# State-space rows turned by a DMA transpose of 16 bit word planes in place of TensorE transposes

## What is computed

```python
x = x + 0.5 * ffn(layernorm(x), W_up, W_gate, W_down)     # ternary weights, silu(up) * gate, 2048 hidden
x = x + mamba(layernorm(x), W_in, conv_w, conv_b, W_out, A_log, D_param, dt_bias)
x = x + 0.5 * ffn(layernorm(x), W_up, W_gate, W_down)
```

```python
S = S * dA_t + dt_t * outer(x_t, B_t)
y_t = S @ C_t
y = (y + D * x) * silu(z)
out = y @ W_out.T
```

## Time and profile before

| | us |
|---|---|
| median of 3 runs | 1743.13 (1742.04 to 1743.46) |
| the profiled execution, its own time | 1743.55 |
| its span, first to last instruction | 1741.8 |
| PE busy | 1707.3 |
| DVE, ACT, POOL busy | 1300.9, 880.5, 743.1 |
| the state-space stage | about 626 to 1135 |

### The profile page before, as it was taken

One profiled execution on the slowest core, in us unless ns is written; L12 is line 12 of the kernel. 1 busy time (PEld: TensorE's weight loads), 2 busy tenths in 40 slices (PEclk: granted clock), 3 DMA queues, 4 the chain that ended last, 5 costly groups with the idle time before them and its releaser, 6 DMA issues. The chain is left out here.

```text
span 1741.8 us, 35220 instructions
## 1 busy us (share of the span) xinstructions
PE 1707.3 (98%) x12992; PEld 1267.0 (73%) x12992; DVE 1300.9 (75%) x2222; ACT 880.5 (51%) x1393; POOL 743.1 (43%) x474
## 2 busy tenths in 40 slices
PE   6999999999999999999999999999999999999999
PEld 3588888888888854444444444646888888888888
DVE  7978777787875758677678667657777787777655
ACT  7755647465473644443434433133647456474553
POOL 2857335253352604435334443534426253352533
PEclk9999999999999999999999999999999999999999
DMA  8032120311214024333423423211130211202100
GB/s 338 25 91 44 48 68 23 90 42 49 51 40 145 0 82 119 116 95 106 129 73 111 136 85 117 87 55 43 49 92 15 76 43 48 68 23 66 43 24 24
DMA packets 135690, 129.90 MB, mean 75 GB/s; under 512 B 105792, under 2 KB 106816, under 8 KB 130240
## 3 DMA queue, kind: packets, MB, share of 16 engines
q1 hardware_dynamic: 135616, 129.04, 23.9%
HBM read 74.75 MB, written 25.43 MB: 58 GB/s over the span
## 5 line engine op out<-in xcount | busy, mean ns | idle before, releaser
L503 POOL TENSOR_TENSOR f_hlo<-f_h,f_hhi 128x768 f16<-128x768 f32 x135 | 201.6, 1493 | 602.1 <-ACT f_hhi L686 573.1
L1260 PE MATMUL f_gate_ps<-spare 128*128 128x256 f16 x2688 | 329.9, 272 | 0.2
L1184 PE MATMUL f_down_ps<-wd,f_hhi 128*128 128x256 fp8e4 x1440 | 318.4, 273 | 0.7 <-DVE xa L881 0.7
L1184 PE MATMUL f_down_ps<-wd,f_hlo 128*128 128x256 fp8e4 x1440 | 318.4, 273 | 0.0
L1260 PEld LDWEIGHTS f_gate_ps<-spare 128*128 128x128 fp8e4 x2688 | 254.7, 97 | 45.2 <-issue 1.9
L1260 PE MATMUL f_up_ps<-spare,wu 128*128 128x256 f16 x1792 | 230.0, 273 | 0.1
L1260 PEld LDWEIGHTS f_up_ps<-spare,wu 128*128 128x128 fp8e4 x1792 | 172.9, 98 | 23.0 <-issue 0.3
L881 DVE SCALAR_TENSOR_TENSOR xa<-f_down_ps,out_scale,xa 128x512 f32<-128x512 f32 x195 | 136.4, 743 | 59.3 <-PE f_down_ps L1184 58.9
L1184 PEld LDWEIGHTS f_down_ps<-wd,f_hhi 128*128 128x128 f16 x1440 | 140.9, 98 | 17.7 <-issue 1.6
L1184 PEld LDWEIGHTS f_down_ps<-wd,f_hlo 128*128 128x128 f16 x1440 | 140.9, 98 | 16.4
L2125 PE MATMUL s_wide<-xnt,late 128*128 128x512 f32 x320 | 146.4, 599 | 4.1 <-ACT xnt L1760 2.8
(11 more groups left out here) (239 smaller groups left out, 3154.2 us busy)
## 6 DMA issues: line engine op xcount, KB each, us to landing
xa<-res SPq DMA_DIRECT2D x16, 1024.0 KB, 6.0
spare<-s_z_rows SPq DMA_DIRECT2D x32, 512.0 KB, 4.3
res<-xa SPq DMA_DIRECT2D x15, 1024.0 KB, 3.9
res<-xa SPq DMA_DIRECT2D x34, 256.0 KB, 2.0
xa<-in_u SPq DMA_DIRECT2D x8, 1024.0 KB, 4.8
xa<-res SPq DMA_DIRECT2D x32, 256.0 KB, 2.7
s_eb<-s_e_rows SPq DMA_DIRECT2D x64, 128.0 KB, 3.1
late<-in_w_gate SPq DMA_DIRECT2D x4, 1024.0 KB, 17.1
```

Of the source, the lines that this page charges most:

```text
L503: last = nc.gpsimd.tensor_tensor(hlo[:, p, a:b, :], src, hhi[:, p, a:b, :], ALU.subtract)
L1184: last = nc.tensor.matmul(at, part[:, p, kind, m * P:(m + 1) * P], wd[:, weight, p, :], start=(p == 0 and part is hhi and (m == 0 or name ...
L1260: last = nc.tensor.matmul(acc[:, j * HT:(j + 1) * HT], w[:, k, e * P:(e + 1) * P], xop[part][:, o, k, :, :], start=(fresh and (j, k, part) ...
```

## The change

For the seven fronts the rows are no longer turned on PE. A DMA transpose handles elements of two bytes, so each float32 is treated as two 16 bit words:

1. ACT's `normal` writes the normalized rows in place, into `xa[:, 2]` (`rows_of`); only BEHIND's go elsewhere, to `zs[:, 0]`. It stands ahead of `gate` in chunk 2 now.
2. POOL's `split_rows` copies the low words and the high words of the rows, two copies of 128x2048 words, into the buffer that the result will have (`xt(f)`), as planes: for each block of 128 features first the low, then the high words.
3. SP's `turn_rows` turns the 4096 words of each partition in blocks of 128x128 with one DMA transpose, back into `xa[:, 2]`.
4. ACT's `join_rows` puts the words together again, two copies of 128x2048 words, into `xt(f)`.

`xt(f)` is `xnt` for the groups of sequence 0 and the old `xn` for those of sequence 1, so there are two buffers. POOL splits in chunk 2 behind `direct`, SP turns in chunk 2 behind `load_chunk`, ACT joins in chunk 3 between `conv_start` and `gate`. For SECOND all of it stands in the opening. `load` of the next rows waits for the join (`xnt_done`) in place of `normal`. BEHIND's transposes stay on PE. The `wide` banks have 12 uses per group in place of 16, with the same order of banks.

```diff
-W_TR, W_BC, W_DTA, W_DT, W_ALL = (0, 1, 2, 3), 4, 5, 6, 16
+W_BC, W_DTA, W_DT, W_ALL = 0, 1, 2, 12
 CONV = (4, 0, 1, 2, 3)
-FIRST, LAST, BEHIND = (0, 0), (GB - 1, 1), (GB, 0)
+FIRST, SECOND, LAST, BEHIND = (0, 0), (0, 1), (GB - 1, 1), (GB, 0)

 def w_conv(f, i):
-    return ((W_BC, 7, 8, 9, 11) if f is LAST else (7, 9, 10, 12, 14) if f is FIRST else (W_BC, 7, 8, 10, 13))[i]
+    return ((W_BC, 3, 4, 5, 7) if f is LAST else (3, 5, 6, 8, 10) if f is FIRST else (W_BC, 3, 4, 6, 9))[i]

 def w_z(f, i):
-    return ((12, 13, 14, 15) if f is LAST else (8, 11, 13, 15) if f is FIRST else (9, 11, 14, 15))[i]
+    return ((8, 9, 10, 11) if f is LAST else (4, 7, 9, 11) if f is FIRST else (5, 7, 10, 11))[i]

 def w_dec(f):
-    return 10 if f is LAST else 12
+    return 6 if f is LAST else 8

...
+def xt(f):
+
+    return xn if f[1] else xnt
+
+def rows_of(f):
+
+    return zs[:, 0, :, :] if f is BEHIND else xa[:, 2, :, :]
+
+def words(ap):
+
+    return ap.bitcast(U16).rearrange("p n (x two) -> p n x two", two=2)
+
+def planes(ap):
+
+    return ap.rearrange("p n x -> p (n x)").bitcast(U16).rearrange("p (k two t) -> p k two t", k=KD, two=2)
...
-            sp.wait_ge(xn_done, after(order(f)))
+            if f is SECOND:
+                sp.wait_ge(xn_done, after(1))
+            else:
+                sp.wait_ge(xnt_done, after(2 * (order(f) - 1)))
             sp.dma_start(xa[:, 2, :, :], out_v[:, bass.ds(tile(f, 0), CH), :]).then_inc(x_in, 16)
+
+        def turn_rows(f):
+
+            sp.wait_ge(split_done, after(2 * order(f)))
+            sp.sem_inc(sp_free, 1)
+            src, dst = (ap.rearrange("p n x -> p (n x)").bitcast(U16) for ap in (xt(f)[:, :, :], xa[:, 2, :, :]))
+            sp.dma_start_transpose(dst.rearrange("p (n t) -> p n t", t=P), src).then_inc(rows_turned, 16)
...
         move_c(FIRST)
+        turn_rows(SECOND)
         keep_rows(FIRST)
...
                     if front is not None:
                         sp.wait_ge(chunks_out, 16 * (CH * order(g) + c))
                         load_chunk(front, c - 1)
+                    if c == CH - 2 and ahead is not None and ahead is not BEHIND:
+                        turn_rows(ahead)
...
+        def split_rows(f):
+
+            if f is SECOND:
+                pool.wait_ge(tr_done, after(KD))
+            else:
+                pool.wait_ge(z_in, after(KD * (order(f) - 1)))
+            pool.wait_ge(xn_done, after(order(f) + 1))
+            pool.sem_inc(pool_free, 1)
+            for w in range(2):
+                nc.gpsimd.tensor_copy(planes(xt(f)[:, :, :])[:, :, w, :].rearrange("p k (c x) -> p c k x", c=CH),
+                                     words(xa[:, 2, :, :])[:, :, :, w].rearrange("p c (k x) -> p c k x", k=KD)).then_inc(split_done, 1)

...
-
-        inv_std((0, 1))
+                if c == CH - 2 and ahead is not None and ahead is not BEHIND:
+                    split_rows(ahead)
+
+        inv_std(SECOND)
+        split_rows(SECOND)
         pool.wait_ge(chan_done, 2)
         pool.wait_ge(scan_done, after(1))
...
-        def copy_transposed(f, k):
-            bank, _ = wide_use(f, W_TR[k])
-            act.wait_ge(tr_done, after(KD * order(f) + k + 1))
-            nc.scalar.activation(xnt[:, k, :], wide[bank][:, :], ACT.Copy).then_inc(wide_free[bank], 1)
+        start_counts(act, [*wide_free, xnt_done, pad_done, xc_done, exp_done, z_done, bt_done, xn_done], done_before)
+
+        def join_rows(f):
+
+            act.wait_ge(rows_turned, 16 * order(f))
+            for w in range(2):
+                nc.scalar.activation(words(xt(f)[:, :, :])[:, :, :, w], planes(xa[:, 2, :, :])[:, :, w, :], ACT.Copy)\
+                  .then_inc(xnt_done, 1)
...
         def normal(f):

             act.wait_ge(nmr_done, after(order(f)))
-            act.wait_ge(tr_done, after(KD * order(f)))
+            if f is BEHIND:
+                act.wait_ge(y4_done, after(CH * order(LAST)))
             for c in range(CH):
-                last = nc.scalar.activation(xn[:, c, :], xa[:, 2, c, :], ACT.Identity,
+                last = nc.scalar.activation(rows_of(f)[:, c, :], xa[:, 2, c, :], ACT.Identity,
                                             bias=nmr[:, c:c + 1], scale=rstd[:, c:c + 1])
             last.then_inc(xn_done, 1)
...
-                if front is not None and c == 0:
-                    for k in range(KD):
-                        copy_transposed(front, k)
                 if (n := next_chunk(g, c, front)) is not None:
...
                         decays(front)
                     conv_end(front, c)
                     conv_start(front, c + 1)
+                    if c == 2 and ahead is not None:
+                        normal(ahead)
+                    if c == CH - 1 and ahead is not None:
+                        join_rows(ahead)
                     if c and front is not LAST:
                         gate(front, c - 1)
                 if g is LAST:
                     gate(g, c)
-                if c == 2 and ahead is not None:
+                if g is LAST and c == 2:
...
-        normal((0, 1))
+        normal(SECOND)
...
         copy_bt(FIRST, 0)
+        join_rows(SECOND)
         gate(FIRST, 3)
...
         def project_conv(f, i, k0=0, k1=KD):
-            if i == 0:
-                taken(pe, f, W_TR[2])
-                taken(pe, f, W_TR[3])
+            if i == 0 and f is not FIRST:
+                pe.wait_ge(xnt_done, after(2 * order(f)))
+                pe.sem_inc(pe_free, 1)
...
-                if front is not None and c == 0:
-                    transposes(front, 0, 2)
-                    turn_x(g, c)
-                    transposes(front, 2, KD)
-                else:
-                    turn_x(g, c)
+                turn_x(g, c)
```

More of the change, by code:

```diff
@@ L20 @@
 F16 = mybir.dt.float16
+U16 = mybir.dt.uint16
 F8 = mybir.dt.float8e4
@@ L1636, in _ @@
                         start_counts(sp, [], done_before)
-                        load((0, 1))
+                        load(SECOND)
                         for c in range(CH):
@@ L1765, in high_parts @@
                             for k in range(k0, k1):
-                                act.wait_ge(tr_done, after(KD * order(BEHIND) + k + 1))
+                                act.wait_ge(tr_done, after(KD + k + 1))
                                 nc.scalar.activation(xhi[:, k], by_tile(behind_bank(k)), ACT.Copy, scale=XS)\
@@ L2103, in product, with transposes @@
                             return wide[bank]
-                        def transposes(f, k0, k1):
+                        def transposes(k0, k1):
                             if k0 == 0:
-                                pe.wait_ge(xn_done, after(order(f) + 1))
+                                pe.wait_ge(xn_done, after(order(BEHIND) + 1))
                             for k in range(k0, k1):
-                                if f is BEHIND and k > 1:
+                                if k > 1:
                                     pe.wait_ge(dtx_done, after(CH * order(LAST) + CH))
@@ L2112, in transposes @@
                                 else:
-                                    acc = product(f, W_TR[k])
+                                    acc = product(BEHIND, k)
                                 for c in range(CH):
-                                    last = nc.tensor.transpose(acc[:, cols(c)], xn[:, c, cols(k)], ident[:, :])
+                                    last = nc.tensor.transpose(acc[:, cols(c)], rows_of(BEHIND)[:, c, cols(k)], ident[:, :])
                                 last.then_inc(tr_done, 1)
                         def project_conv(f, i, k0=0, k1=KD):
-                            if i == 0:
-                                taken(pe, f, W_TR[2])
-                                taken(pe, f, W_TR[3])
+                            if i == 0 and f is not FIRST:
+                                pe.wait_ge(xnt_done, after(2 * order(f)))
+                                pe.sem_inc(pe_free, 1)
                             acc = product(f, w_conv(f, i)) if k0 == 0 else wide[wide_use(f, w_conv(f, i))[0]]
@@ L2124, in project_conv @@
                             for k in range(k0, k1):
-                                last = nc.tensor.matmul(acc[:, :], win[:, k, row:row + P], xnt[:, k, :],
+                                last = nc.tensor.matmul(acc[:, :], win[:, k, row:row + P], xt(f)[:, k, :],
                                                         start=(k == 0), stop=(k == KD - 1))
@@ L2135, in project_dta @@
                             for k in range(KD):
-                                last = nc.tensor.matmul(acc[DTW * k:DTW * (k + 1), :], win[:, k, 0:DTW], xnt[:, k, :],
+                                last = nc.tensor.matmul(acc[DTW * k:DTW * (k + 1), :], win[:, k, 0:DTW], xt(f)[:, k, :],
                                                         start=True, stop=True, skip_group_check=True)
@@ L2276, in group @@
                                 elif g is LAST:
```

(4 more changed lines are left out.)

13 lines of the change are left out of this document (8 added, 5 removed).

## The result

The changed kernel takes 1746.99 us in the median (14 runs, 1744.69 to 1748.89), the kernel before 1742.83 beside it on the same chip (14 runs, 1741.99 to 1743.46). The ratio is 1.0021, with an interval of 1.0015 to 1.0028: 4.2 us slower, where the forecast was 2.7 slower, with 3.5 as the bound of what counts as no change. The runs scatter three times as widely as before. The execution profiled took 1745.48 with a span of 1743.7, so it shows 1.9 of the 4.2 us: it is one of the quicker ones, and the other 2.3 are in executions without a trace.

What follows compares the result with a forecast made beforehand. TensorE, busy 98% of the span, was taken as the bound. -14.1 + 7.2 + 5.4 + 4.2 = +2.7 us on the profiled 1743.55; against the median, forecast 1745.8 us (+0.15%), range 1732 to 1762.

Steps and rivals of the forecast that it cites:

- the gap ahead of the decay matmul: Sign on PE: a gap of about 1.2 us, 2.5 in the opening, released by DVE's a32.
- rival C: Next group's stats on DVE wait for the load, z rows late too: 1 to 2 us x 6, 1755; chance 0.08.
- The removed transposes: Each front gives back up to 2.35 us on PE; six in the steady state, 14.1 saved.
- a32 late by the copies: POOL's splits hold up DVE's softplus steps, so TensorE waits 1.2 us before turn_decays; +7.2 in six groups.
- T: Time of each POOL split copy: taken as 2.0 us, range 1.9 to 4.15.
- Rival A: Faster: POOL's copies do not block DVE, or only what has slack; 12.3 us saved, 1731; chance 0.32.
- Taps onto inner: DVE's taps come 2.35 us earlier and wait for POOL's inner; PE 0.9 later per group, +5.4 in six.
- The rest of the chain in steady groups: DMA transpose, joins and SP's queue in steady groups: hidden, nothing added; the transfer with over 6 us to spare.
- The scaling: DMA transpose of 4096 words, scaled from 3584: 4.1 us of SP's queue and 5.8 to landing.
- The opening: SECOND's splits and joins delay z, the scans and first chunk_y; +4.2 us, nothing gained from removed transposes there.

Runs made afterwards that it cites:

- e2: Changed kernel without GpSimd's two copies, the joins writing zeros: 1743.64 us, ratio 1.0007 to the kernel before.
- e10: Changed kernel with the next rows' load issued early by ScalarE, without GpSimd's two copies (joins write zeros): 1735.62 us, ratio 0.9955.
- e3: Changed kernel with a third GpSimd copy of the same size ahead of the two: 1766.01 us, ratio 1.0136.
- e11: Changed kernel with the next rows' load issued early by ScalarE, and a third GpSimd copy: 1758.93 us, ratio 1.0089.
- e8: Changed kernel without copies, DMA transpose and joins (stale rows), the next rows' load issued early by ScalarE: 1732.26 us, ratio 0.9934.
- e7: Changed kernel with SECOND turned by TensorE in the opening and the next rows' load issued early by ScalarE: 1735.92 us, ratio 0.9958.
- e6: Changed kernel with the next rows' load issued by ScalarE as the group opens, instead of by SP: 1740.24 us, ratio 0.9981.
- e12: Changed kernel with ScalarE's early load, SECOND's joins moved behind the last gate and SiLU in the opening: 1739.85 us, ratio 0.9978.
- e5: Changed kernel with SP issuing the next rows' load ahead of the z rows' broadcast for chunk 2: 1740.44 us, ratio 0.9982.
- e4: Changed kernel with SECOND turned by TensorE in the opening, without the new chain for it: 1743.17 us, ratio 0.9999.
- e9: Kernel before the change, with only the next rows' load issued by ScalarE as the group opens: 1746.77 us, ratio 1.0023.

## Why the prediction was right, and where it was not

The sign and the rough size are right: +2.7 forecast, +4.2 measured, which is beyond the forecast's own bound of 3.5 and so the outcome "slower", given 0.40. Of its signs, the gap ahead of the decay matmul came four times too small in the groups and as 1.74 rather than 2.5 in the opening, and the sign of rival C, DVE waiting for xa, came too. The copies' price and the load's were wrong by about 6 us each, in opposite directions, the taps' was 1.9 too high and the opening's 1.5 too low.

- **The removed transposes, 2.35 in each opening:** right. PE goes from S to the projection in 0.77 us. 6 x 2.35 = 14.1.
- **a32 late by the copies, 1.2 in each of six groups, 7.2:** right in mechanism, four times too large: 0.21 to 0.29, 1.6 in total. The forecast let the copies end 4.45 after direct and five steps of 0.22 follow. They run back to back in 3.73, which is 0.7 sooner. And its own pattern, one step in between any two POOL instructions, has a further step caught behind the second copy, which the forecast did not count: that step ends with the copy, and four follow, 0.2 sooner. What is left of 1.2 is the 0.3 measured. T itself was taken right (1.89 for 2.0). The Trainium skill (SBUF — State Buffer, Who interferes with whom) has a two-input DVE instruction wait for all of a GpSimd instruction that reads SBUF and was issued first. Here that holds for a one-input copy and steps of 0.2: e2 and e10 take the waits away, e3 and e11 lengthen them by a copy. Of the two rows that the forecast read it from, the one at 749.99 is a TENSOR_SCALAR with one input, of which this rule does not speak; the steps at 765.77 have two. Rival A (no lock) is wrong, though its price was nearly right for this term.
- **Taps onto inner, 0.9 in each group, 5.4:** right in mechanism. The taps take 1.0 longer (4.20). They take as long in e8 (4.21), which has no chain and no late load, and what it costs shows there: the ideal period is 62.40 - 2.35 = 60.05 and it has 60.75, so 0.7 a group, over five periods 3.5. That all of the 0.7 is the taps is read from the timelines; no run took their overlap with inner away.
- **The rest of the chain in steady groups, nothing:** right within the 0.34 of e7 against e8, which is the a32 wait. The mis-sized transfer and join (6.7 and 2.49 each) stay hidden. ACT waits 0.1 for the planes in each group, and 0.6 and 0.7 once each in e6 and e11, where the forecast had none. The scaling failed: 4096 words are 1.14 times 3584, and took 1.35 times as long on the queue and 1.31 times to land as in the forecast's row.
- **The opening, +4.2:** the place was right (the joins ahead of the last SiLU on ACT; by e12 their length costs, not their order), the size too small. The SiLU starts 6.7 later (667.32 for 660.59), 1.0 of it because the joins take 4.83 and not 3.8. The lower clock after the gap adds 2.8, for which the forecast had no term, and the transposes that no longer stand behind the SiLU, with the waits around them, give 2.1 back, where the forecast took nothing. So chunk_y comes 7.4 later. 1.7 comes back within the first group, whose own waits vanish, so 5.7 net.
- **Rival C, the load:** wrong in weight, and this is the step that failed. "Stats for the next group wait on a load that now leaves SP with 0.6 us of slack in place of 1.5" was true in kind; it had a chance of 0.08 and no term in the sum, as if a slack of 0.6 were no wait. The slack is 7.2 - 7.0 = 0.2 against the median landing, and the landing goes to 8.8. DVE, in order, hands each us on to its dtx, and PE waits 1.6 to 1.9 for that in three groups of the profile and, from the 6.5 of e5, in more of them in the median run.

The parts add up on the profiled execution. Up to the last front's projection: -14.1, + 5.7 for the opening and the first group, + 3.5 for the taps, + 5 x 0.34 = 1.7 for the chain, + 4.6 for three late loads (1.64 + 1.70 + 1.91, less the 0.2 each that is there anyhow) is +1.4; measured +1.5 (1042.08 for 1040.54). With 6.5 for the loads the median would be +3.3, 0.9 short of the measured 4.2. In other executions a late load's wait may bring the clock down as well, as in e4; the changed kernel's one profile does not show it.

So the forecast hit because 7.2 + 5.4 + 4.2 = 16.8 and 1.7 + 3.5 + 5.7 + 6.5 = 17.4 are nearly the same sum. The mechanisms of its terms were right; that the errors in their sizes make up for the missing load is luck. What stays open is why this load lands in 5.2 us in one group and in 8.8 in another (that the broadcast ahead of it has a part is what e5 suggests), and why the clock falls at one gap of 1.9 and not at the next.

## What to carry to other kernels

When work at the head of a stage is taken away, list every transfer whose issue stays where it was while its reader comes sooner, and compare its longest landing, not its median, with what is left; then move the issue up with the change, as e5 does with one line. Count a long gap on TensorE twice: once as a wait, once as the lower clock of the work behind it (here 6.28 and 2.8; at 1.9 in some groups 1.7 more). A chain that is hidden in the steady state is not hidden in the one-time opening; there the old way (e4) can be kept.

## What the runs showed of the hardware

- ScalarE takes 2.49 us for 128x2048 words of 16 bits written at a stride of two, against 1.91 for 2048 elements from f32 to f16 written densely.
- A GpSimd copy of 128x2048 words read at a stride of two takes 1.89, less than its product of two inputs that makes 1024. Two back to back take 3.73, and each holds one of DVE's small two-input steps to its own end (1.80 for a step of 0.19), with the next step caught by the next copy. The pattern seen before the change, that one gets in between any two, held.
- A DMA transpose within SBUF of 4096 words a partition holds SP's queue for 4.85 and lands in 6.7, against 3.58 and 5.1 for 3584 words.
- Gaps of 1.8 to 1.9 us on TensorE were followed by the lower clock in four groups of e11 and not in the other two, at a cost of 1.7 us each; one of 2.73 was in e9. Three of 1.64 to 1.91 in the changed kernel's profile were not.
